# Queries' stack on GpSimd, values on ScalarE with their bias in x, scores by query one place sooner

## The reference, cut to what matters

```python
q = einsum('oc,bcn->bno', Wq, xf) + bq          # 16 query channels
k = einsum('oc,bcn->bon', Wk, xf) + bk[:, None]
v = einsum('oc,bcn->bon', Wv, xf) + bv[:, None]
attn = softmax(einsum('bnd,bdm->bnm', q, k) / sqrt(16), axis=-1)
out = einsum('bcm,bnm->bcn', v, attn)
x = gamma[0] * out + x
```

## Time and profile before

| what | value |
|---|---|
| median of three runs | 552.88 us (549.94 to 553.61) |
| time of the profiled execution | 552.03 us |
| its span | 550.1 us |
| mean granted TensorE clock | 0.901 |
| PE busy | 460.2 us (84%) |
| DVE busy | 316.8 us (58%) |
| ACT busy | 191.7 us (35%) |
| POOL busy | 158.7 us (29%) |

### The profile page before, as it was taken

How to read it: one execution, slowest core, us unless ns; L and a number is a source line. 1 busy time by engine, 2 the same in 40 slices (tenths; PEclk the granted TensorE clock), 3 DMA queues, 4 the chain that set the end, 5 groups by cost and what they waited for, 6 DMA issues and landing times.

```text
span 550.1 us, 9237 instructions
## 1 busy us (share of the span) xinstructions
PE 460.2 (84%) x2929; PEld 397.3 (72%) x2929; DVE 316.8 (58%) x871; ACT 191.7 (35%) x398; POOL 158.7 (29%) x168
## 2 busy tenths in 40 slices
PE   5879999998889988899875847987778689999847
PEld 3449667887657976578864646987677689999747
DVE  3854687467746569455647734656533345555436
ACT  3060534516217243134133403452222234444343
POOL 1000000100623202504107331335666554444500
PEclk9668999998969989879956986988998989999969
DMA  6800100001100002100001001212222222222187
GB/s 195 281 2 0 39 0 2 1 2 38 41 20 11 12 0 83 45 1 21 1 16 63 15 21 40 55 40 65 64 65 68 63 63 60 69 60 70 41 235 229
DMA packets 28869, 30.21 MB, mean 55 GB/s; under 512 B 5074, under 2 KB 24146, under 8 KB 28696
## 3 DMA queue, kind: packets, MB, share of 16 engines
q1 hardware_dynamic: 24248, 20.09, 13.1%
q0 software_dynamic: 4576, 9.53, 5.1%
HBM read 17.44 MB, written 12.16 MB: 54 GB/s over the span
## 4 chain that ended last, share of the span: by engine, by line
PE 61%; DVE 16%; issue 7%; another core or an unknown queue 5%; ACT 5%; DMA 3%; POOL 1%; SPq 1%; DVEq 0%; POOLq 0%; ACTq 0%
PE bank_c L372 25%; PE bank_s L372 19%; PE bank_a L372 9%; DVE row_max_sb L899 3%; PE bank_c L643 3%; DVE values_sb L960 3%; PE bank_a L622 1%; PE bank_c L443 1%; DVE v_ext_sb L892 1%; DMA probs_sb<-xs_dram 1%; ACT probs_sb L744 1%; DMA y_dram<-probs_sb 1%; DVE ln_sb L932 1%; PE bank_a L507 1%
## 5 line engine op out<-in xcount | busy, mean ns | idle before, releaser
L1363 POOL DMA_INDIRECT y_dram<-probs_sb x71 | 68.0, 957 | 83.8 <-ACT probs_sb L835 80.0
L1331 POOL DMA_INDIRECT xs_dram<-ln2x_sb,slots_sb x64 | 64.7, 1011 | 63.9 <-DVE slots_sb L1064 45.6
L1323 POOL TENSOR_TENSOR rstd_sb<-var_eps_sb,minus_half_sb 128x4 f32<-128x4 f32 x16 | 16.4, 1022 | 195.1 <-DVE var_eps_sb L926 195.1
L774 ACT ACTIVATE values_sb<-bank_s,g_head_sb 128x1024 fp32r<-128x1024 f32 x32 | 35.3, 1113 | 90.9 <-PE bank_s L372 59.7
L372 PE MATMUL bank_c<-v_ext_sb,probs_sb 128*128 128x129 f32 x512 | 62.5, 283 | 4.8 <-issue 3.5
L372 PEld LDWEIGHTS bank_c<-v_ext_sb,probs_sb 128*128 128x128 f32 x512 | 60.9, 198 | 6.7 <-issue 6.7
L372 PE MATMUL bank_c<-values_sb,wp_hi_sb 128*128 128x256 f32 x256 | 59.6, 310 | 0.0
L899 DVE TENSOR_REDUCE row_max_sb<-bank_a 128x1 f32<-128x512 f32 x64 | 41.5, 685 | 27.5 <-remote 14.3
L372 PE MATMUL bank_s<-probs_sb,x_hi_sb 128*128 x142 | 53.4, 376 | 2.9 <-issue 1.4
L372 PEld LDWEIGHTS bank_c<-values_sb,wp_hi_sb 128*128 128x128 f32 x256 | 46.9, 211 | 5.7 <-issue 4.7
L372 PE MATMUL bank_s<-probs_sb,x_lo_sb 128*128 x142 | 47.1, 331 | 0.0
(11 more groups left out here) (189 smaller groups left out, 915.8 us busy)
## 6 DMA issues: line engine op xcount, KB each, us to landing
probs_sb<-xs_dram SPq DMA_DIRECT2D x71, 66.0 KB
probs_sb<-y_dram SPq DMA_DIRECT2D x16, 256.0 KB, 5.2
w_rest_sb<-in_w_dram SPq DMA_DIRECT2D x1, 2728.0 KB, 12.6
xc_sb<-in_x_dram SPq DMA_DIRECT2D x4, 512.0 KB, 3.3
y_dram<-probs_sb POOLq DMA_INDIRECT x71
xs_dram<-ln2x_sb,slots_sb POOLq DMA_INDIRECT x64
xs_dram<-pads_sb SPq DMA_DIRECT2D x1, 528.0 KB, 7.4
wq_s_sb<-in_wq_dram SPq DMA_DIRECT2D x1, 512.0 KB, 3.9
```

The costliest lines, as they stand in the source:

```text
L774: nc.scalar.activation(vh_hi[:, hd % RING, :], bank_s[hd % 2][:, :], ACT.Copy, scale=g_head[:, hd:hd + 1]).then_inc(vh_high, 1)
L1323: G.tensor_tensor(rstd[:, tiles], var_eps[:, tiles], minus_half[:, tiles], ALU.pow).then_inc(rstd_ready, 1)
L1331: G.indirect_dma_start(xs_dram, bass.IndirectOffsetOnAxis(ap=slots[:, i, k:k + 1], axis=0), ln2x[:, k // TILES, k % TILES, :], None).then_ ...
L1363: G.indirect_dma_start(y_dram, bass.IndirectOffsetOnAxis(ap=x_rows[k][:, C:C + 1].bitcast(I32), axis=0), y_rows[k], None).then_inc(scatter ...
```

## The change

Three things are changed. (1) DVE keeps only the keys' stack (`make_k_stack`). POOL makes the queries' stack (`make_q_stack`) in two instructions of 32 rows, a subtraction and a copy, with a wait between them. PE waits for `q_ready` and `k_ready` before the first scores. (2) ACT keeps the values (`keep_v`, now a scaled copy of each half) behind `keep_ln1T`. The bias `gbv` is added to `xt` by one POOL instruction over 128x1024 (`add_v_bias`), and DVE's first `attended` of an image waits for it. (3) In PE's `image` each pair of scores stands one place sooner, the first of them before `head_values(i, 1)`; on DVE the first `row_max` stands before the first `low_head_values`, and `set_slots(i-1)` before `head_weights`. In POOL's `image` the two new functions stand behind the first two reciprocal roots and ahead of the scatters; for image 0 they stand behind the last rewriting of the padding rows.

```diff
--- before.py
+++ after.py
@@ -256,13 +256,13 @@
         def ranking(i):
             return (A[0], bank_a[0]) if i == IMAGES - 1 else (S[0], bank_s[0])
 
-        stack_step, max_step = sem("stack_step"), sem("max_step")
+        q_ready, k_ready, xt_ready, max_step = sem("q_ready"), sem("k_ready"), sem("xt_ready"), sem("max_step")
         norm_step, gate_step = sem("norm_step"), sem("gate_step")
         rstd_ready, exp_ready = sem("rstd_ready"), sem("exp_ready")
         ids_added, ln2_copied = sem("ids_added"), sem("ln2_copied")
         xs_stored = [sem(f"xs_stored{i}") for i in range(IMAGES)]
         pads_made, surplus_stored, pads_placed, pads_stored = sem("pads_made"), sem("surplus_stored"), sem("pads_placed"), sem("pads_stored")
...
         LN1_STEP, SECOND_STEP, BOTH_STEP, SLOT_STEP = 8, 6, 11, 15
         LN2_STEP = (12, 16)
         setup, den_ready, tok_step = sem("setup"), sem("den_ready"), sem("tok_step")
@@ -399,7 +399,8 @@
             def scores_by_query(i, n):
 
                 if n == 0:
-                    pe.wait_ge(stack_step, i * STACK_STEPS + (STACK_STEPS + 1))
+                    pe.wait_ge(q_ready, 2 * i + 2)
+                    pe.wait_ge(k_ready, i + 1)
                 for h in range(2):
                     pe.wait_ge(A[h].drained, A[h].before(i, "scores", n))
                     mm(bank_a[h][:, :], q_stack[0:STACK, n * P:(n + 1) * P],
@@ -563,25 +564,25 @@
 
                 head_values(i, 0)
                 head_sums(i)
+                beside(0)
                 head_values(i, 1)
-                beside(0)
+                beside(1)
                 head_values(i, 2)
                 biases(i)
-                beside(1)
+                beside(2)
                 head_values(i, 3)
-                beside(2)
+                beside(3)
                 project_heads(i, 0, range(0, 5))
-                beside(3)
+                beside(4)
                 project_heads(i, 0, range(5, HEADS))
                 head_values(i, 4)
-                beside(4)
+                beside(5)
                 head_values(i, 5)
-                beside(5)
+                beside(6)
                 project_heads(i, 1, range(0, 5))
-                beside(6)
+                beside(7)
                 project_heads(i, 1, range(5, HEADS))
                 head_values(i, 6)
-                beside(7)
                 head_values(i, 7)
                 if not last:
                     max_rows(i + 1)
@@ -719,7 +720,9 @@
                 for h in range(2):
                     act.wait_ge(A[h].filled, A[h].full(i, "qk"))
 
-                    act.wait_ge(stack_step, i * STACK_STEPS + 1)
+                    if i > 0:
+                        act.wait_ge(q_ready, 2 * i)
+                        act.wait_ge(k_ready, i)
                     nc.scalar.activation(qk_hi[:, h * HALF:(h + 1) * HALF], bank_a[h][:, :], ACT.Identity, bias=vec_s[:, 0:1])
                     nc.scalar.activation(qk_sum[:, h * HALF:(h + 1) * HALF], bank_a[h][:, :], ACT.Identity,
                                          bias=vec_s[:, 0:1]).then_inc(A[h].drained, 1)
@@ -731,6 +734,12 @@
                         act.wait_ge(Cb[h].drained, Cb[h].after(i - 1, "pv", K - 1))
                     act.wait_ge(A[h].filled, A[h].full(i, "xt"))
                     nc.scalar.copy(xt[:, 4 * h:4 * h + 4, :], bank_a[h][:, :].rearrange("p (n c) -> p n c", c=C)).then_inc(A[h].drained, 1)
+
+            def keep_v(i):
+                for h in range(2):
+                    act.wait_ge(A[h].filled, A[h].full(i, "v"))
+                    nc.scalar.activation(v_ext[:, 4 * h:4 * h + 4, 0:C], bank_a[h][:, :].rearrange("p (n c) -> p n c", c=C), ACT.Copy,
+                                         scale=vec_s[:, 1:2]).then_inc(A[h].drained, 1)
 
             def max_rows(i):
                 for h in range(2):
@@ -801,6 +810,8 @@
                     stack_sums(i + 1)
                     keep_xt(i + 1)
                 keep_ln1T(i)
+                if not last:
+                    keep_v(i + 1)
                 keep_head_values(i)
                 if not last:
                     max_rows(i + 1)
@@ -809,6 +820,8 @@
 
             stack_sums(0)
             keep_xt(0)
+            act.wait_ge(consts_made, 3)
+            keep_v(0)
             keep_wv()
             max_rows(0)
             for m in range(TILES):
@@ -878,20 +891,12 @@
             def bcast_e(ap):
                 return ap.unsqueeze(2).broadcast_to([P, TILES, EXPERTS])
 
-            def make_stacks(i):
+            def make_k_stack(i):
                 for h in range(2):
                     dve.wait_ge(A[h].drained, A[h].after(i, "qk"))
-                for k, (dst, lo) in enumerate(((q_stack, 0), (k_stack, STACK))):
-                    rows = slice(lo, lo + STACK)
-                    V.scalar_tensor_tensor(out=dst[0:STACK, :], in0=qk_hi[rows, :].bitcast(F32), scalar=cst_s[rows, C_LOW:C_LOW + 1],
-                                           in1=qk_sum[rows, :], op0=ALU.mult, op1=ALU.add).then_inc(stack_step, 1)
-
-            def keep_v(i):
-                for h in range(2):
-                    dve.wait_ge(A[h].filled, A[h].full(i, "v"))
-                    V.scalar_tensor_tensor(out=v_ext[:, 4 * h:4 * h + 4, 0:C], in0=bank_a[h][:, :].rearrange("p (n c) -> p n c", c=C),
-                                           scalar=vec_s[:, 1:2], in1=gbv[:].unsqueeze(1).broadcast_to([P, 4, C]),
-                                           op0=ALU.mult, op1=ALU.add).then_inc(A[h].drained, 1)
+                rows = slice(STACK, 2 * STACK)
+                V.scalar_tensor_tensor(out=k_stack[0:STACK, :], in0=qk_hi[rows, :].bitcast(F32), scalar=cst_s[rows, C_LOW:C_LOW + 1],
+                                       in1=qk_sum[rows, :], op0=ALU.mult, op1=ALU.add).then_inc(k_ready, 1)
 
             def row_max(i, n):
                 for h in range(2):
@@ -910,6 +915,8 @@
             def attended(i, n):
 
                 c = Cb[n % 2]
+                if n == 0:
+                    dve.wait_ge(xt_ready, i + 1)
                 dve.wait_ge(c.filled, c.full(i, "pv", n // 2))
                 s0 = (i * TILES) + n
                 V.reciprocal(rden[:, n:n + 1], bank_c[n % 2][:, C:VCOLS]).then_inc(den_ready, 1)
@@ -1154,35 +1161,33 @@
                     keep_ranks(i - 1)
                 low_lnT(i)
                 if not last:
-                    make_stacks(i + 1)
+                    make_k_stack(i + 1)
+                if not first:
+                    set_slots(i - 1)
                 head_weights(i)
-                if not last:
-                    keep_v(i + 1)
 
                 def beside(n):
                     if not last:
                         row_max(i + 1, n)
 
+                beside(0)
                 low_head_values(i, 0)
-                beside(0)
-                if not first:
-                    set_slots(i - 1)
                 if last:
                     early_table()
+                beside(1)
                 low_head_values(i, 1)
-                beside(1)
+                beside(2)
                 low_head_values(i, 2)
-                beside(2)
+                beside(3)
                 low_head_values(i, 3)
                 if last:
                     split_w13(0)
                 keep_bias(i)
-                beside(3)
                 beside(4)
+                beside(5)
                 low_head_values(i, 4)
-                beside(5)
+                beside(6)
                 low_head_values(i, 5)
-                beside(6)
                 beside(7)
                 if not last:
                     negate_max(i + 1)
@@ -1205,14 +1210,12 @@
             V.memset(k_stack[STACK:STACK + 2, :].bitcast(F32), 1.0).then_inc(consts_made, 1)
             for bank in (*A, *S, *Cb):
                 dve.sem_inc(bank.drained, 1)
-            dve.sem_inc(stack_step, 1)
             dve.wait_ge(loaded["wqk"], 48)
             dve.wait_ge(loaded["cst"], 32)
             dve.wait_ge(loaded["wv"], 32)
             V.tensor_scalar(gbv[:], bvB_s[:], vec_s[:, 1:2], None, ALU.mult).then_inc(consts_made, 1)
             dve.wait_ge(consts_made, 4)
-            make_stacks(0)
-            keep_v(0)
+            make_k_stack(0)
             for n in range(TILES):
                 row_max(0, n)
             negate_max(0)
@@ -1322,6 +1325,22 @@
                 pool.wait_ge(norm_step, i * NORM_STEPS + step_ready)
                 G.tensor_tensor(rstd[:, tiles], var_eps[:, tiles], minus_half[:, tiles], ALU.pow).then_inc(rstd_ready, 1)
 
+            def make_q_stack(i):
+                for h in range(2):
+                    pool.wait_ge(A[h].drained, A[h].after(i, "qk"))
+                if i > 0:
+                    pool.wait_ge(rstd_ready, 4 * (i - 1) + 2)
+                high, low = slice(0, 2 * DQK), slice(2 * DQK, STACK)
+                G.tensor_tensor(q_stack[low, :], qk_sum[low, :], qk_hi[low, :].bitcast(F32), ALU.subtract).then_inc(q_ready, 1)
```

(15 more changed lines are left out.)

2 lines of the change are left out of this document (1 added, 1 removed).

## The result

Measured beside each other in 20 runs each, the kernel after takes 559.32 us in the median (555.21 to 562.43) and the kernel before 551.61 (543.90 to 556.89). The ratio is 1.0171, 95% interval 1.0138 to 1.0204: slower by 1.7%. The forecast was 559, slower by over 1% with a chance of 0.48. The profiled execution of after took 562.43 us (span 560.5) against 552.03 (550.1) before, so the two traces differ by 10.4 us, the medians by 7.7.

The account below looks back on a forecast made before the run. PE, busy 84% and 61% of the chain, was taken as the main bound, alternating with DVE at the start. Terms 10.6 + 1.2 - 1.0 - 3.4 - 0.85 = +6.55 us on 552.03 gave 558.6, forecast 559 us, range 550 to 565.

Parts of the forecast that it names:

- the 5.25 us of gains: Heads' part of all images: 1.0 us in image 0, 3.4 in images 1 and 2 together, 0.85 in image 3.
- the forecast's own case: Whole kernel: the forecast's terms hold, time from 556.5 to 561.5 us; chance 0.47.
- The start, +10.6: Image 0's start: POOL's queries stand behind the padding's store, so first scores come 10.6 us later (9.6 to 12.5).
- The clock, +1.2: Image 0's eight score pairs: PE, idle before, runs them at the slower clock; 1.2 us lost (0 to 1.2).
- Values on ACT, 0: Image 0's start: ACT keeping the values costs nothing, since scores wait for POOL some 10 us longer.
- image 0's heads, -1.0: Image 0's heads: PE's waits of 1.55 us go, a new one of about 0.5 remains; 1.0 us gained.
- images 1 and 2, -1.7 each: Heads of images 1 and 2: image 0's terms plus PE's 0.80 us before head 3; 1.7 us gained each.
- the wait before head 2: Image 0's heads: PE has a new wait of about 0.5 us because DVE frees head 0's bank later.
- Image 3, -0.85: Image 3's heads: `set_slots` moves off the path into DVE's idle time before `qsum`; 0.85 us gained.
- the second rival: Heads and start: gains hidden or given back by earlier scatters or POOL's bias holding up DVE's keys, loss stays; 566 us, chance 0.15.
- The gaps did not go away (0.15): Rival, heads of images 1 and 2: earlier scatters remove the gaps with no sender, 14 us at most; 545 us, chance 0.15.
- The start did not cost less (0.2): Rival, image 0's start: padding's store lands sooner and pairs run at full clock, 3 us less; 556 us, chance 0.2.

Follow-up runs that it names:

- A late start alone: The kernel before with one added wait: DVE makes image 0's stacks only after the padding rows' store; 535.43 us, ratio 1.0190.
- second pair of traces: Both kernels run and traced again, no edit, on a chip without gaps: after 533.02 us, ratio 1.0157; before 522.51 us, ratio 0.9964.
- the kernel with the queries first: The kernel after, with image 0's queries' stack and bias on POOL ahead of the wait for the padding's store; 522.64 us, ratio 0.9971.
- The kernel with the queries behind the norm: The kernel with the queries first; later images' queries on POOL also wait until DVE has normalised all pixels; 520.23 us, ratio 0.9924.
- the scatters late: The kernel with the queries first, the first 12 scatters waiting for ACT's head 4; 525.30 us, ratio 1.0019.
- both stacks on DVE: The kernel after, but DVE makes queries' and keys' stacks in every image and POOL only the bias, behind the keys; 528.19 us, ratio 1.0082.
- the new order alone: The kernel before with only the third part's order of scores, row maxima and slots, values still on DVE; 532.65 us, ratio 1.0021.
- the order undone: The kernel with the queries behind the norm, scores, row maxima and slots put back in the order of before; 523.98 us, ratio 0.9993.
- the start's queries on DVE: The kernel with the queries behind the norm, image 0's queries' stack made on DVE again; 522.57 us, ratio 0.9944.

## Why the prediction was right

**The number.** That 559 and 559.32 agree to 0.3 us is luck. The sum was +6.55 us on a base of three runs, 552.88; twenty runs put the base at 551.61, and the difference measured is 7.7 us by the medians, 9.4 by the ratio and 10.3 to 10.4 between traces. The start is right in mechanism and size; of the 5.25 us of gains little is left: after is 12.6 us behind at the first attended pixels of image 0 and 10.4 at the end in the first pair of traces, 11.0 and 10.3 in the second. The upper end of the forecast's own case, 561.5, is also 1 us more than its bounds give (558.6 + 1.9 = 560.5); nothing hangs on it.

**The start, +10.6.** Right by its mechanism and within 0.4 us by its size: first scores +10.94 (24.96 - 14.02). POOL's pair took 2.33 + 1.03 where 1.95 + 0.98 was the estimate from the memset; the halved figure of the page GPSIMD Engine Reference of the Trainium skill (section Performance versus the Vector engine), 2.25 us, was the nearer. A late start alone costs 1.9%, and its removal takes the change from 1.0157 to 0.9971, so this term is the result. (The two ratios are of two sessions, each against the kernel before in its own.)

**The clock, +1.2.** The eight pairs all ran at 0.50. To the weighing's start it came to 12.79 - 10.94 = 1.85. What I left out is that the clock comes back sooner in the weighing, which returned 1.13 us. Net 0.7. In the second pair of traces this term is nothing: first scores +11.02 (24.96 - 13.94), weighing +10.92 (51.45 - 40.53). There the kernel before was itself at half the clock from 16 us on.

**Values on ACT, 0; image 0's heads, -1.0; images 1 and 2, -1.7 each.** Where the clock stayed full and no gap fell in, the terms are right: -0.9 in image 0 (35.73 against 36.59) and -1.9 in image 1 of the second pair, with the wait before head 2 at 0.42 where I had 0.5. The order brought them, not the two instructions freed from DVE (0.2 us). And they did not reach the end: in the second trace of after, in the session without gaps, image 1 kept its 1.9 and image 2 lost 2.0. There PE runs at half the clock (from 217 to 228 us), as the stretches of 4 us show for the kernel with the queries first, image 1's heads and image 2's:

```profile
136.00:140.00 4.00, 4.00 (x22) 2.89 (x22) 2.45 (x7) 1.49 (x2) 3.09 (x4) 1.00 0.37 132
...
204.00:208.00 4.00, 4.00 (x11) 2.15 (x12) 3.85 (x9) 2.23 (x2) 3.09 (x4) 0.70 0.48 185
208.00:212.00 4.00, 4.00 (x11) 2.75 (x10) 2.25 (x4) 1.11 (x1) 3.09 (x4) 0.50 0.27 95
```

The same work, 38.3 us in one image, takes 42.3 in the other. The kernel with the queries behind the norm has such spells in images 0 and 1 and not in image 2. Added up over the first 350 us, the time at half the clock is 65 us in the kernel before and 89 in the kernel after in the second pair of traces (11 of the 24 more lie in the start), 85 and 96 in the first pair, and 75 to 92 in the ten variants. That these spells eat the order's gain is shown by the stretches. That the new order brings more of them is likely by the mean granted clocks of the runs that the ratios count: 0.9125 with the queries first and 0.911 with the scatters late, against 0.920 for the kernel before beside them; 0.9055 with both stacks on DVE and 0.905 with the new order alone, against 0.919; but 0.918 with the order undone, against 0.918. With the queries behind the norm the distance is small (0.918 against 0.920; 0.915 against 0.918 with the start's queries on DVE). Why the spells fall on one image and not on another is open.

**Image 3, -0.85.** Right: the counts behind the slots stood 3.87 us behind `qsum` (289.79 - 285.92) and now stand 3.03 behind it (296.11):

```profile
299.14 0.14 DVE L1112 TENSOR_TENSOR counts_i_sb<-base_sb,regions_sb 1x8 int32<-1x8 f32 x1
```

The first pair of traces gives -1.6 from image 3's weighing to its experts' stage, the second -1.7 (-1.79 from `qsum`, +0.09 before it). What goes beyond 0.84 there was no step of mine; both traces of after have less time at half the clock between image 3's first attended pixels and the experts (21 against 28 us, 22 against 24).

**What the sum lacked.** POOL's queries and DVE's norm did not run at once: +2.0 us of VectorE in image 0. The stretch to `qsum` grew by 0.1 us in the first pair of traces and 0.7 in the second, but the time at half the clock in it differs too (1.7 us before and none after in the first pair), so neither number is the price of the hold. The bias held the keys' stack as well, 1.60, 1.45 and 1.74 us in images 0, 1 and 2 against 1.28. I had priced POOL's instructions by their own length and asked who waits for their results, and did not ask what they hold while they run. Only the second rival spoke of DVE being held, through the order of the queue and not through the memory. The Trainium skill has the rule, on the page GPSIMD Engine Reference, section Key points: GpSimd and VectorE share their interfaces to SBUF and contend when the VectorE instruction has two SBUF inputs or runs in a two-port mode. The runs agree for the instructions listed at the end, and add the size: the whole of the other instruction.

**The rivals.** The gaps did not go away (0.15): they stayed with their place in the schedule and not with the scatters, though in this one pair of traces only. The start did not cost less (0.2). Gains hidden with the loss kept at 566 (0.15) was half true: part of the gains was hidden, by the clock, but the part from image 3's `qsum` on gave back 3.3 us in the second pair. Of these 0.84 are the slots'; 1.5 fall in the experts' stage (201.17 to 199.69 us from its first step to the end), which the change leaves alone and in which the trace of after has 15.5 us at half the clock against 20.4. The kernel with the queries behind the norm has 20.4 us there and takes 201.22. The rest, some 0.9, goes with the 1.8 us less at half the clock ahead of the experts. So that part is the clock's, and luck for the change.

**Better than both.** The kernel with the queries first and behind the norm, 0.9924 (0.9884 to 0.9964) in its session, 0.5% by the medians. Against the yardstick of 0.9964 for the same kernel that is a gain of some 0.4 to 0.8% at best, from one session; it was not run again, and its cause is not shown.

## What to carry to other kernels

When an operation moves to another engine, read that engine's program from the top: an idle engine (29% busy here) that stands in a wait when the operand is ready costs the whole wait. The place in the queue (11 us), not the length of the instructions (3.36 us), set this result. Then look at what runs on VectorE in the time of every SBUF instruction given to GpSimd, and put that GpSimd instruction beside VectorE instructions that read PSUM; here that took the holds away, and what it is worth in time is not settled. A gain in one stage counts only when the stage is compared at the same granted clock, and a baseline timed against itself gives the size under which no variant is a win.

## What the runs showed of the hardware

- These pairs of a GpSimd instruction on SBUF and a VectorE instruction did not run together; one waited for the rest of the other. Beside GpSimd's subtraction or bias of 2.3 to 2.4 us, a VectorE `tensor_scalar` of 128x128 from SBUF to SBUF took 2.37 us instead of 0.34, the keys' stack (two SBUF inputs) 3.48 instead of 1.28, an addition of 128x8 (two SBUF inputs) 1.96 instead of 0.17, a cast of 128x16 from SBUF to SBUF 1.92 instead of 0.17. In the other direction GpSimd's copy took 1.91 instead of 1.03, and its bias, begun 0.2 us behind the keys' stack, 3.30 instead of 2.38.
- These were not held: VectorE instructions that read PSUM (1.28 us beside the bias, row maxima 0.69 each), and a `tensor_reduce` from SBUF to SBUF (128x128 to 128x16, 0.29 and 0.28 us in the middle of the bias, at 134.97 and 209.50 in the kernel with both stacks on DVE).
- GpSimd on 1024 fp32 columns: a two-input operation 2.33 us (32 partitions) and 2.38 (128 partitions), a copy 1.03.
- The same program on the same chip took 523 us in one session and 546 in another. The chains of the two variants traced in the second have waits with no sender, 6% of the span; their cause stays open, and so does the placing of the half-clock spells. In one session the same program took 521 to 524 us at a mean granted clock of 0.915 to 0.928 and 525 to 527 at 0.906 to 0.912.
